# Attention with the row maximum carried by one fp32 product, two buffers for it, and copies and sums at other places in the order

## The reference

```python
q = (x @ Wq.T + bq).reshape(B, L, H, hd)      # rope on q and k follows
scores = jnp.einsum('bqhd,bkhd->bhqk', q, k) / np.sqrt(hd)
attn = jax.nn.softmax(scores, axis=-1)
out = jnp.einsum('bqhk,bkhd->bqhd', attn, v)  # then @ Wo.T + bo
```

## Time and profile before

| | us |
|---|---|
| median of 3 runs | 5297.65 (5293.94 to 5299.45) |
| profiled execution | 5298.74 |
| its span, first to last instruction | 5296.9 |
| TensorE busy | 4559.5 (86%) |
| VectorE busy | 3727.4 (70%) |
| GpSimd busy | 2562.3 (48%) |
| ScalarE busy | 2326.3 (44%) |

### The profile page before, as it was taken

How to read it: one execution, slowest core, us unless ns; L and a number is a source line. 1 busy time by engine, 2 the same in 40 slices (tenths; PEclk the granted TensorE clock), 3 DMA queues, 4 the chain that set the end, 5 groups by cost and what they waited for, 6 DMA issues and landing times. The chain is left out here.

```text
span 5296.9 us, 82808 instructions
## 1 busy us (share of the span) xinstructions
PE 4559.5 (86%) x25792; PEld 2900.2 (55%) x25792; DVE 3727.4 (70%) x4809; ACT 2326.3 (44%) x3747; POOL 2562.3 (48%) x1341
## 2 busy tenths in 40 slices
PE   6689999968888588888888888888885775999999
PEld 6678888846666322222222222222223664888888
DVE  6667777667787677777777777777763886777776
ACT  4433333322232155555555555555553443333332
POOL 2334444345665355555555555555554554344443
PEclk9999999979999799999999999999997887999999
DMA  4465555344444633433333334433323654555552
GB/s 134 140 199 174 172 176 169 107 146 151 147 146 136 155 67 88 88 88 84 81 81 86 88 86 88 88 87 81 81 63 105 189 161 124 183 172 177 171 175 90
DMA packets 450425, 664.71 MB, mean 125 GB/s; under 512 B 190336, under 2 KB 191616, under 8 KB 450240
## 3 DMA queue, kind: packets, MB, share of 16 engines
q1 hardware_dynamic: 409280, 596.01, 40.8%
q0 software_dynamic: 40960, 66.65, 4.0%
HBM read 502.77 MB, written 178.33 MB: 129 GB/s over the span
## 5 line engine op out<-in xcount | busy, mean ns | idle before, releaser
L1474 POOL TENSOR_TENSOR att_pairsum<-att_p,att_p 128x1024 f32<-128x1024 f32 x512 | 1204.7, 2375 | 1029.0 <-ACT att_p L1492 550.8
L1547 DVE TENSOR_REDUCE att_big<-att_mx 128x2 f32<-128x2048 f32 x512 | 1174.3, 2293 | 625.5 <-PE att_mx L1601 617.1
L1492 ACT ACTIVATE att_p<-att_st 128x512 f32<-128x512 f32 x2048 | 1141.0, 598 | 914.6 <-PE att_st L1623 840.7
L1623 PE MATMUL att_st<-att_q,att_k 128*128 128x512 f32 x2048 | 907.1, 486 | 89.6 <-ACT att_p L1492 72.4
L1623 PEld LDWEIGHTS att_st<-att_q,att_k 128*128 128x128 f32 x2048 | 351.8, 191 | 810.9 <-ACT att_p L1492 538.3
L1633 PE MATMUL att_op<-att_p,att_v 128*32 128x512 f32 x4096 | 600.9, 661 | 1.6 <-ACT att_p L1492 1.0
L845 DVE TENSOR_TENSOR e_w<-e_raw,e_w 128x2048 fp32r<-128x2048 f32 x192 | 439.4, 2290 | 9.8 <-ACT e_w L840 5.8
L863 ACT ACTIVATE e_sg<-e_gp 128x324 f32<-128x324 f32 x256 | 113.3, 443 | 632.2 <-PE e_up L176 617.3
L840 ACT ACTIVATE e_w<-e_raw 128x2048 fp32r<-128x2048 f32 x192 | 366.4, 1909 | 55.6 <-DMA e_raw<-in_w_gate 47.9
L1601 PE MATMUL att_mx<-att_mk,att_mq 32*128 32x512 f32 x2048 | 264.9, 505 | 124.1 <-DVE att_big L1547 104.5
L899 DVE SCALAR_TENSOR_TENSOR e_xg<-e_yp,e_meta,e_xg 108x512 f32<-108x512 f32 x192 | 144.2, 751 | 314.7 <-PE e_yp L176 314.7
(11 more groups left out here) (146 smaller groups left out, 9013.2 us busy)
## 6 DMA issues: line engine op xcount, KB each, us to landing
e_raw<-in_w_gate SPq DMA_DIRECT2D x64, 1024.0 KB, 5.7
e_raw<-in_w_up SPq DMA_DIRECT2D x64, 1024.0 KB, 9.5
e_raw<-in_w_down SPq DMA_DIRECT2D x64, 1024.0 KB
att_q<-q SPq DMA_DIRECT2D x192, 256.0 KB, 4.1
att_k<-k SPq DMA_DIRECT2D x192, 256.0 KB, 6.2
att_mq<-q SPq DMA_DIRECT2D x128, 256.0 KB, 7.7
r_x<-in_x SPq DMA_DIRECT2D x16, 1024.0 KB
x<-r_base SPq DMA_DIRECT2D x16, 1024.0 KB, 9.7
```

The source lines that it names most:

```text
L1474: nc.gpsimd.tensor_tensor(out=pairsum[h][g % 2][:, :], in0=pr[h][2 * g % RING][:, :], in1=pr[h][(2 * g + 1) % RING][:, :], op=ALU.add).the ...
L1492: nc.scalar.activation(pr[h][kt % RING][:, c * HALF:(c + 1) * HALF], st[c][:, :], ACT.Exp, scale=SCALE).then_inc(s_exp, 1)
L1547: nc.vector.tensor_reduce(out=big[:, :, qt], in_=mx[:, :, :, :].rearrange("p h c k -> p h (c k)"), axis=AX.X, op=ALU.max).then_inc(s_max, 1)
L1623: nc.tensor.matmul(st[c][:, :], kst[b][:, h, kt * P:(kt + 1) * P], qst[b][:, h, c * HALF:(c + 1) * HALF], start=True, stop=True).then_inc( ...
```

## The change

The split into two bf16 parts and the bf16 identity go. `big` gets the layout that `parts` had (maximum in column 0, zeros in the 31 others), in fp32 and twice, by the parity of the pair; the row product takes `big` and the fp32 `ident`. ScalarE copies o, z and the row after x = 1 instead of x = 2, and the two halves of its row copy come at kt = 4 and 5 instead of both at 4. On TensorE, totals 0 and 1 move from kt = 5, 6 to kt = 6, 7; at kt = 2 the totals, and at kt = 4 the row, come in front of the products.

```diff
+    TOTALS = {KT - 2: 0, KT - 1: 1, 0: 2, 2: 3}
-        identb = sb("identb", [P, P], BF16)
-        big = sb("big", [P, 2, KT])
-        parts = sb("parts", [P, 2, KT, HD], BF16)
+        big = S.pair(sb, "big", [P, 2, KT, HD])
...
-            nc.gpsimd.memset(parts[:, :, :, :], 0.0).then_inc(s_memset, 1)
+            for par in range(2):
+                nc.gpsimd.memset(big[par][:, :, :, :], 0.0).then_inc(s_memset, 1)
...
-            def copy_row(i, b):
+            def copy_row(i, b, c):
                 act.wait_ge(s_row, DEPTH * i + b + 1)
-                for c in range(2):
-                    nc.scalar.activation(qst[b][3 * HD:4 * HD, 1, half(c)], zp[tile(1, c), :],
-                                         ACT.Copy).then_inc(s_rowq[1], 1)
+                nc.scalar.activation(qst[b][3 * HD:4 * HD, 1, half(c)], zp[tile(1, c), :],
+                                     ACT.Copy).then_inc(s_rowq[1], 1)
...
-                        if last and (kt, x) == (0, 2):
+                        if last and (kt, x) == (0, 1):
                             copy_o(*last)
-                        if last and (kt, x) == (2, 2):
+                        if last and (kt, x) == (2, 1):
                             copy_z(*last)
-                        if left and (kt, x) == (ROW, 2):
-                            copy_row(*ahead(i, b, 1))
+                        if left and kt in (ROW, ROW + 1) and x == 1:
+                            copy_row(*ahead(i, b, 1), kt - ROW)
...
-            nc.vector.tensor_copy(identb[:, :], ident[:, :]).then_inc(s_identb, 1)
...
                 if qt == 0:
-                    dve.wait_ge(s_mlo, p)
-                nc.vector.tensor_reduce(out=big[:, :, qt], in_=mx[:, :, :, :].rearrange("p h c k -> p h (c k)"),
+                    dve.wait_ge(s_row, past(p - 1))
+                nc.vector.tensor_reduce(out=big[b % 2][:, :, qt, 0], in_=mx[:, :, :, :].rearrange("p h c k -> p h (c k)"),
                                         axis=AX.X, op=ALU.max).then_inc(s_max, 1)
-
-            def split(i, b):
-
-                p = DEPTH * i + b
-                dve.wait_ge(s_max, KT * (p + 1))
-                dve.wait_ge(s_row, p)
-                nc.vector.tensor_tensor(out=parts[:, :, :, 0], in0=big[:, :, :], in1=big[:, :, :],
-                                        op=ALU.max).then_inc(s_mhi, 1)
-                dve.wait_ge(s_mhi, p + 1)
-                nc.vector.tensor_tensor(out=parts[:, :, :, 1], in0=big[:, :, :], in1=parts[:, :, :, 0],
-                                        op=ALU.subtract).then_inc(s_mlo, 1)
...
-                    split(*ahead(i, b, 1))
...
-                pe.wait_ge(s_mhi, p + 1)
-                pe.wait_ge(s_mlo, p + 1)
+                pe.wait_ge(s_max, KT * (p + 1))
                 pe.wait_ge(s_zo, past(p - 1))
                 for t in range(KT // 2):
                     for h in range(2):
                         for c in range(2):
-                            last = nc.tensor.matmul(zp[tile(h, c), t * P:(t + 1) * P], parts[:, h, c * (KT // 2) + t, :],
-                                                    identb[:, :], start=True, stop=True)
+                            last = nc.tensor.matmul(zp[tile(h, c), t * P:(t + 1) * P], big[b % 2][:, h, c * (KT // 2) + t, :],
+                                                    ident[:, :], start=True, stop=True)
...
                 for kt in range(KT):
+                    if kt == 2 and before:
+                        totals(p - 1, TOTALS[kt], left)
+                    if kt == ROW and left:
+                        row(*nxt)
                     if kt > 0:
                         products(p, b, kt - 1)
                     elif before:
                         products(p - 1, (b - 1) % DEPTH, KT - 1)
-                    if kt in (0, 2) and before:
-                        totals(p - 1, 2 + kt // 2, left)
-                    if kt == ROW and left:
-                        row(*nxt)
-                    if kt in (ROW + 1, ROW + 2):
-                        totals(p, kt - ROW - 1, left)
+                    if kt == 0 and before:
+                        totals(p - 1, TOTALS[kt], left)
+                    if kt >= KT - 2:
+                        totals(p, TOTALS[kt], left)
```

More of the change, by code:

```diff
@@ L1376, in attention @@
         s_memset = sem("s_memset")
-        s_identb = sem("s_identb")
         s_in = [sem(f"s_in{b}") for b in range(DEPTH)]
@@ L1380, in attention @@
         s_max = sem("s_max")
-        s_mhi = sem("s_mhi")
-        s_mlo = sem("s_mlo")
         s_row = sem("s_row")
@@ L1462, in _ @@
         def _(pool):
-            nc.gpsimd.memset(parts[:, :, :, :], 0.0).then_inc(s_memset, 1)
+            for par in range(2):
+                nc.gpsimd.memset(big[par][:, :, :, :], 0.0).then_inc(s_memset, 1)
             nc.gpsimd.memset(ones[:, :], 1.0).then_inc(s_memset, 1)
-            pool.wait_ge(s_memset, 2)
+            pool.wait_ge(s_memset, 3)
             for b in range(DEPTH):
@@ L1522, in step @@
                         exps(p, kt, x)
-                        if last and (kt, x) == (0, 2):
+                        if last and (kt, x) == (0, 1):
                             copy_o(*last)
-                        if last and (kt, x) == (2, 2):
+                        if last and (kt, x) == (2, 1):
                             copy_z(*last)
-                        if left and (kt, x) == (ROW, 2):
-                            copy_row(*ahead(i, b, 1))
-            copy_row(0, 0)
+                        if left and kt in (ROW, ROW + 1) and x == 1:
+                            copy_row(*ahead(i, b, 1), kt - ROW)
+            for c in range(2):
+                copy_row(0, 0, c)
             rounds_by(DEPTH, act, NP, step)
@@ L1537, in _ @@
             dve.wait_ge(s_const, 16)
-            dve.wait_ge(s_memset, 2 + DEPTH)
-            nc.vector.tensor_copy(identb[:, :], ident[:, :]).then_inc(s_identb, 1)
+            dve.wait_ge(s_memset, 3 + DEPTH)
             def maxima(i, b, qt):
@@ L1579, in _ @@
                 maxima(0, 0, qt)
-            split(0, 0)
             copy_row(0, 0)
@@ L1588, in _ @@
             pe.wait_ge(s_const, 16)
-            pe.wait_ge(s_memset, 2 + DEPTH)
-            pe.wait_ge(s_identb, 1)
+            pe.wait_ge(s_memset, 3 + DEPTH)
             def rough(i, b, qt):
```

## The result

The changed kernel takes 5061.5 us (median of 4 runs, 5055.99 to 5068.54) against 5296.2 before: ratio 0.9557, 95% interval 0.9541 to 0.9574. The forecast was 4994 in 4970 to 5080. The sign and the range held; of the 304 us promised, 235 came, and the 68 us that are missing have one cause, a stall where TensorE's loop goes back to its start, which the sum had put at nothing.

What follows compares the result with a forecast made beforehand. It took attention's head pairs to be bound by TensorE's key steps, with 5.9 of 34.10 us stall. New pair 29.15, gain 4.95 over 63 steps, 312 less 7.5 less 1, giving 4994 us, range 4970 to 5080.

Steps and rivals of the forecast that it cites:

- The split is what the row and the next reduction wait for: VectorE's split, 4.57 us a pair, makes the row product wait 1.5 us and delays the next reduction; removing it ends both.
- S3 to S4: Fourth of eight key steps in a head pair, timed between score starts, holding the row product: 5.01 us to become 3.97.
- S4 to S5: Key step after the row's: 6.88 us to become a plain 3.10, losing its wait, totals and clock fall.
- The fp32 row costs 0.86 to 0.87 of TensorE's time: Row product priced like the fp32 totals, 0.86 us; by four passes through the array it would be 1.36.
- rival 2: The fp32 row's matmuls do not overlap: 3.9 us instead of 0.87, giving 5185 us; chance 0.06.
- The copies are hidden behind x = 1: ScalarE's copies of o and z fit its idle time there; S0-S1 and S2-S3 lose about 0.5 us each, becoming 3.10.
- Row copies with 0.3 and 0.2 us of slack: After the row, VectorE's copies finish 0.3 us before its next reduction, ScalarE's second 0.2 before its exponential: no wait.
- rival 1: Those VectorE and ScalarE slacks are missing, costing 0.5 to 1.5 us a pair; at 1.0, 5057 us; chance 0.14.
- Totals at 6 and 7 cost nothing: Totals 0 and 1 move a key step later; S6-S7 grows from 3.10 to 3.96, GpSimd's later adds cause no wait.
- The clock comes back: In S4 to S5 TensorE's thin stretch goes, and with it the clock's fall to 0.57; granted clock near 1.00 throughout.
- The loop's back edge costs 7.5 us: At the loop's return, one pair in four, the copy of o stays unhidden: 0.5 us for 15 pairs.
- Sixteen bf16 matmuls become sixteen fp32 ones: Term pricing the row product's change to fp32 on TensorE: 0.86 to 0.87 us, bounds 0.34 and 3.9.

Runs made afterwards that it cites:

- experiment 4: Kernel before with only the split removed: one fp32 row product in 4 wide matmuls, two buffers, old order on TensorE and ScalarE; 5184.3 us, ratio 0.9793.
- experiment 7: Kernel before with the split's first instruction a copy of one input instead of a maximum of two; 5294.6 us, ratio 1.0001.
- experiment 6: Kernel with 4 wide row matmuls, one piece put back each time: o and z copies 5054.9 us, row copy in one piece 5090.7, totals at kt 5, 6 5035.5.
- Experiments 4 and 5: The second of these: kernel before with split and bf16 row kept, only the new order on TensorE and ScalarE's copies; 5246.1 us, ratio 0.9894.
- wide_row: Changed kernel with the row product as 4 fp32 matmuls of 128 stationary columns instead of 16 of 32; 4989.7 us, ratio 0.9425.

## Why the prediction was right, and which term was missing

- *The split is what the row and the next reduction wait for.* Right: in the changed kernel S3 to S4 is 3.98 and S4 to S5 3.09, predicted 3.97 and 3.10; the second of these needs the new order too (experiment 4 has 4.01 and 5.30). Its length of 2.3 us an instruction was put down to two SBUF inputs beside GpSimd's adds; one input is held as long (experiment 7), so it doesn't take two.
- *The fp32 row costs 0.86 to 0.87 of TensorE's time.* Right: 0.89 from its start to the products'. The four passes over the bf16 time, 1.36, did not come, so the totals were the better row to price it by; rival 2 (3.9) is out.
- *The copies are hidden behind x = 1.* Right: 3.09 and 3.11 for 3.10, and 65 us when put back (experiment 6).
- *Row copies with 0.3 and 0.2 us of slack.* 0.17 and 0.20 measured; rival 1 did not come, by a thin margin, which is luck as much as judgement.
- *Totals at 6 and 7 cost nothing.* Right, and better than left alone: at 5 and 6 they wait for ScalarE's copy, 46 us (experiment 6), which the sum had not claimed.
- *The clock comes back.* Right, 1.00 in the pair. But the prediction took it for a by-product of the wait that goes with the split. Experiments 4 and 5 show that it needs both halves: each alone leaves a gap and, in half of the pairs or more, a low stretch, and 143 of 305 us appear only together.
- *The loop's back edge costs 7.5 us.* The prediction saw ScalarE's late exponential there and priced a copy that isn't hidden, for 15 pairs. There are 13 returns, and in wide_row the pair with a return takes 0.54 us more than the others, 7 us in all: that part came. What the sum had at nothing is the stall: in the changed kernel each return costs 5.5 us more than in wide_row. Four pairs take 122.7 us in the changed kernel (2081.31 to 3553.74, from one idle gap to the twelfth after it) and 117.2 in wide_row (2077.71 to 3249.83, from ScalarE's late exponential to the tenth after it). That is 72 us. The step that missed it is "Sixteen bf16 matmuls become sixteen fp32 ones": it counted columns and time, and even counted the records for their start rate, but never as length of the loop. Its sum for everything else, 4994, was met by wide_row at 4990, where the same work stands in fewer records.

Not tried: the limit between 0 and 64 records more exactly; a row product in another engine; the gap of 1.35 us with other work before or behind it, to see what lowers the clock.

## What to carry to other kernels

Count what an edit adds to the code of a hardware loop, not only its time: on the engine with the longest body, 64 records more were enough for a loss of 5 us at nearly every return, and a matmul of plain fp32 counts double (eight records for the four of `products`; a score in fp32r, the rounded form, has one). Tiles that share their moving operand can be one wide matmul: here 4 instead of 16 at the same length, worth 72 us. Two edits that each remove one of two gaps in the same step can be worth nearly twice their sum (305 us against 162 here) when TensorE's clock hangs on it, so judge them together.

## What the runs showed of the hardware

- A TensorE loop grown from 1408 records to 1472 or 1536 shows it in three places: nine packets of 16.4 KB on the instruction queue in each round (65 in all become 173 or 183), an idle gap of mostly 3.1 to 3.6 us (twice 4.3) at the return, and 1.2 GHz behind it (1.94 us for products of 1.06). It is near to a step: half of the growth costs 60 of 77 us at the returns.
- A VectorE instruction of 16 elements for each partition takes 2.3 us beside GpSimd's adds of 2.37 us and 0.20 to 0.23 without, whether it reads one SBUF operand or two.
- A gap of 1.34 us on TensorE, in the same place of every pair of one kernel, was followed by full speed in about half of the pairs and by a lowered clock in the others (1.06 and up to 1.94 us for the same products); with another order around it, a gap of 1.35 us left 58 of 63 at full speed.
